# Experts of a decoder: the second norm moved into the middle stage, and the expert loop reordered

## The reference, cut to what matters

```python
scores = softmax(xf @ gate_w.T)                 # xf: 4096 x 128, the output of a layer norm
vals, idx = top_k(scores.T, k)                  # k = 512 tokens for each of 8 experts
y = xf[flat_idx].reshape(k, n, d)
mu = y.mean(-1, keepdims=True)
var = ((y - mu) ** 2).mean(-1, keepdims=True)
y = (y - mu) * rsqrt(var + LN_EPS) * ln_w + ln_b   # the second norm
h = gelu(einsum('knd,nfd->knf', y, fc1s) + b1s)
out = (einsum('knf,ndf->knd', h, fc2s) + b2s) * kept_w[..., None]
xf = xf.at[flat_idx].add(out.reshape(k * n, d))
```

## Time and profile before

| what | us |
|---|---|
| median of 3 runs (3424.35 to 3433.75) | 3430.83 |
| the profiled execution's own time | 3433.34 |
| its span, first to last instruction | 3430.7 |
| busy in the span: PE / DVE / ACT / POOL | 2574.6 / 1733.4 / 1027.6 / 342.9 |
| middle stage, one pass in its steady part | 103 |
| experts, first gather (1465.30) to the first load of the sum (1613.77) | 148.5 |

### The profile page before, as it was taken

The page is one execution under the profiler, slowest core; times in us unless marked ns, Lnnn a source line. Parts: engine busy times, 40 slices in busy tenths (PEclk is TensorE's granted clock), DMA queues, the critical chain, the costliest instruction groups (busy, mean ns, idle before and its releaser), DMA issues.

```text
span 3430.7 us, 54304 instructions
## 1 busy us (share of the span) xinstructions
PE 2574.6 (75%) x22608; PEld 1834.1 (53%) x22608; DVE 1733.4 (51%) x4213; ACT 1027.6 (30%) x1406; POOL 342.9 (10%) x580
## 2 busy tenths in 40 slices
PE   4666358888988886366777789777797777977778
PEld 3444146777777675244655454554545545454454
DVE  5555744566665654621367541575415754157540
ACT  3333422222222221021132442324423244232442
POOL 0111000000000000064111000110001100011000
PEclk8788658999999998588898999989999899998999
DMA  2000000000000001013700000000000000000000
GB/s 80 0 0 0 2 1 1 8 7 8 1 8 8 8 7 50 42 31 51 183 2 1 1 7 1 1 1 1 7 1 1 1 1 7 1 1 1 1 1 25
DMA packets 39364, 48.16 MB, mean 14 GB/s; under 512 B 7170, under 2 KB 36370, under 8 KB 38355
## 3 DMA queue, kind: packets, MB, share of 16 engines
q1 hardware_dynamic: 33490, 40.43, 4.0%
q0 software_dynamic: 5632, 4.33, 0.9%
HBM read 31.81 MB, written 12.91 MB: 13 GB/s over the span
## 4 chain that ended last, share of the span: by engine, by line
PE 42%; issue 32%; DVE 17%; POOL 4%; ACT 3%; DMA 1%; POOLq 0%; DVEq 0%; SPq 0%; ACTq 0%
PE banks L2332 6%; PE banks L861 5%; PE banks L2530 3%; PE banks L1361 2%; PE banks L1326 2%; PE banks L1160 2%; DVE weights L2053 2%; DVE xs L890 1%; PE banks L560 1%; PE banks L1394 1%; PE banks L2321 1%; POOL rstd L899 1%; PE banks L1106 1%; PE banks L1171 1%; PE banks L1952 1%
## 5 line engine op out<-in xcount | busy, mean ns | idle before, releaser
L2530 PE MATMUL banks<-wA 128*128 128x128 f32 x2234 | 302.2, 289 | 0.0
L2530 PEld LDWEIGHTS banks<-wA 128*128 128x128 f32 x2234 | 283.6, 203 | 15.0 <-issue 14.0
L882 DVE BATCH_NORM_STATS2 stats<-banks 128x6 f32<-128x128 f32 x208 | 46.3, 285 | 333.8 <-PE banks L861 295.2
L2224 DVE TENSOR_REDUCE wide_area<-banks 128x8 f32<-128x2048 f32 x64 | 146.6, 2291 | 102.9 <-PE banks L2144 102.9
L2196 ACT ACTIVATE weights<-banks 128x2048 f32<-128x2048 f32 x64 | 120.1, 1877 | 121.4 <-PE banks L2157 121.4
L897 POOL TENSOR_TENSOR rstd<-moments,eps 128x4 f32<-128x4 f32 x56 | 11.2, 201 | 1396.0 <-DVE moments L886 1396.0
L1717 DVE TENSOR_REDUCE wide_area<-banks 128x16 f32<-128x1024 f32 x80 | 94.1, 1218 | 54.1 <-PE banks L1630 53.8
L882 DVE BATCH_NORM_STATS2 dilvals<-banks 128x6 f32<-128x128 f32 x144 | 32.0, 285 | 174.6 <-PE banks L861 174.6
L890 DVE TENSOR_SCALAR xs<-banks,moments,rstd 128x128 f32<-128x128 f32 x208 | 71.0, 403 | 39.8 <-POOL rstd L899 39.3
L2332 PE MATMUL banks<-wide_area,big 128*128 128x512 f32 x192 | 86.3, 592 | 0.0
L922 ACT ACTIVATE xf<-banks 128x256 f32<-128x256 f32 x64 | 24.1, 384 | 205.8 <-PE banks L911 205.2
(11 more groups left out here) (746 smaller groups left out, 6165.9 us busy)
## 6 DMA issues: line engine op xcount, KB each, us to landing
big<-in_wE SPq DMA_DIRECT2D x1, 4096.0 KB, 12.5
weights<-long_kernel SPq DMA_DIRECT2D x8, 512.0 KB, 7.4
conv<-wide_area SPq DMA_DIRECT2D x16, 256.0 KB, 3.2
wC<-in_wC SPq DMA_DIRECT2D x1, 3012.0 KB, 17.4
wC<-in_wG SPq DMA_DIRECT2D x1, 2971.0 KB, 18.7
big<-in_wT SPq DMA_DIRECT2D x1, 2560.0 KB, 11.7
x_all<-in_xT SPq DMA_DIRECT2D x1, 2048.0 KB, 11.0
rows<-spread SPq DMA_DIRECT2D x8, 256.0 KB, 2.5
```

Of the source, the lines that this page charges most:

```text
L882: dve.bn_stats(m.stats[:, i, :], self.tokens(i)).then_inc(*sg.up("dve", f"stats{i}"))
L2224: dve.tensor_reduce(m.peaks[:, k % 2, :, :].rearrange("p t (r c) -> p r t c", r=4)[:, :, :, SPARE[j]], bank[:, :, :].rearrange("p r (t k) ...
L2530: pe.matmul(bank[:, 0:P], m.ident, m.ident, start=True, stop=True)
```

## The change

The second norm is taken out of the expert loop. In the middle stage a new class `LaneRows` makes the factor of the second norm from the moments of the first: a token that left the first norm has mean zero (taken as exactly zero now) and variance var x rstd x rstd. Four small operations on POOL make (var x rstd x rstd + eps) to the power -1/2, a fifth multiplies the tile of 512 tokens by it into `rows_normed`, and SP stores that into `rows_dram` in place of `far.xs`. `total_dram` still gets `far.xs`, now first. The lead lane's norm on DVE waits until POOL has read the moments that the two lanes share.

In the expert loop, `moments`, `root`, `scaled` and the copy of gate values are gone; `features` transposes the gathered rows themselves, and `weighted` reads the gate value from them. There are six buffers for gathered rows instead of three, five gathers are issued before the first add and one behind each of the first three adds. PE's order is features(0), features(1), hidden(0), hidden(1), features(2), and then `out(e)`, `hidden(e+2)`, `features(e+3)`, so that between the hidden layer of an expert and its output stands the work of another. ACT's order follows that. Twenty and five fillers stand before features(0) and features(1).

```diff
@@ class Experts
-    BUFFERS = 3
+    BUFFERS = 6
+    AHEAD = 5
...
+    def landed(self, e):
+        return self.gathered[e % self.BUFFERS], 16 * NT * (e // self.BUFFERS + 1)
...
         def gather(e):
             if e >= self.BUFFERS:
-                pool.wait_ge(*tk.done("dve", "weight", e - self.BUFFERS))
+                pool.wait_ge(*rs.done("dve", f"weighted{NT - 1}", e - self.BUFFERS))
...
-        def root(e):
...
-        gather(0)
-        gather(1)
-        root(0)
-        gather(2)
-        root(1)
+        for e in range(self.AHEAD):
+            gather(e)
         for e in range(EXPERTS):
-            if e + 3 < EXPERTS:
-                gather(e + 3)
-            if e + 2 < EXPERTS:
-                root(e + 2)
             add(e)
+            if self.AHEAD + e < EXPERTS:
+                gather(self.AHEAD + e)
...
         def features(e):
-            pe.wait_ge(*tk.done("dve", f"scaled{NT - 1}", e))
+            pe.wait_ge(*self.landed(e))
...
-        for e in range(2):
-            features(e)
-            hidden(e)
+        m.keep_busy(pe, m.S[0][:, 0, :], "taken")
+        features(0)
+        m.keep_busy(pe, m.S[0][:, 0, :], "chosen")
+        features(1)
+        hidden(0)
+        hidden(1)
+        features(2)
         for e in range(EXPERTS):
             out(e)
             if e + 2 < EXPERTS:
-                features(e + 2)
                 hidden(e + 2)
+            if e + 3 < EXPERTS:
+                features(e + 3)
...
+        affine(0)
+        affine(1)
+        gelu(0)
+        gelu(1)
+        affine(2)
+        for e in range(2, EXPERTS):
+            gelu(e)
+            if e + 1 < EXPERTS:
+                affine(e + 1)
...
-        def moments(e):
...
-        def scaled(e):
...
+                dve.tensor_scalar(m.weighted[e % 2][:, i, :], m.PT[:, e % 2, i * P:(i + 1) * P], self.taken(e)[:, i, D + e:D + e + 1],
                                   None, ALU.mult).then_inc(*rs.up("dve", f"weighted{i}"))
...
+class LaneRows:
+        self.sig = Section(clock, pool="part var eps root rows")
+    def pool(self, pool, n, scaled, written):
+        m, sg = self.lane, self.sig
+        pool.wait_ge(*scaled)
+        pool.tensor_tensor(self.factor, m.moments[:, :, 1], m.rstd, ALU.mult).then_inc(*sg.up("pool", "part"))
...
+        pool.tensor_tensor(self.factor, self.factor, m.rstd, ALU.mult).then_inc(*sg.up("pool", "var"))
...
+        pool.tensor_tensor(self.factor, self.factor, m.eps4[:, :], ALU.add).then_inc(*sg.up("pool", "eps"))
...
+        pool.tensor_tensor(self.factor, self.factor, m.minus_half[:, :], ALU.pow).then_inc(*sg.up("pool", "root"))
+        pool.wait_ge(*sg.done("pool", "root", n))
+        pool.wait_ge(*written)
+        pool.tensor_tensor(self.rows, m.xs, self.factor.unsqueeze(2).broadcast_to([P, NT, D]), ALU.mult).then_inc(*sg.up("pool", "rows"))
...
         def lead_dve(dve, it):
             yield from lead_down.dve(dve, it, m.big[:, :, bass.ds(it * T, T)])
+            if later(it, 2):
+                dve.wait_ge(*far_rows.sig.done("pool", "var", it - 2))
             yield from lead_norm.dve(dve, it, lead_down.z_ready(it))
...
             yield from far_norm.pool(pool, it)
+            far_rows.pool(pool, it, far_norm.sig.done("dve", f"scaled{NT - 1}", it), (saved, it * 48 + 16))
             yield from far_gate.pool(...)
...
             def store_rows(it):
                 sp.wait_ge(*far_norm.sig.done("dve", f"scaled{NT - 1}", it))
-                for dst, row in ((rows_dram, Experts.ROW), (total_dram, D)):
-                    sp.dma_start(..., far.xs[:, :, :]).then_inc(saved, 16)
+                sp.dma_start(bass.AP(total_dram.tensor, ...), far.xs[:, :, :]).then_inc(saved, 16)
+                sp.wait_ge(*far_rows.sig.done("pool", "rows", it))
+                sp.dma_start(bass.AP(rows_dram.tensor, ...), rows_normed).then_inc(saved, 16)
                 sp.wait_ge(*far_gate.sig.done("dve", "prob", it))
```

More of the change, by code:

```diff
@@ L494, in __init__ @@
         self.rows, self.total = rows, total
-        self.take = Signals(ctx, nc, "take", dve=tile_steps("stats", "aggr", "scaled") + " weight", pool="eps rstd", pe="features",
-                            act="out")
+        self.take = Signals(ctx, nc, "take", pe="features", act="out")
         self.hid = Signals(ctx, nc, "hidden", pe="h0 h1 h2 h3", act="g0 g1 g2 g3")
@@ L600, in gelu, with dve @@
                                bias=self.b1[:, e * FC + c:e * FC + c + 1]).then_inc(*hd.up("act", f"g{c}"))
-        for e in range(EXPERTS):
[L603 to L607, removed]
-        def moments(e):
[L610 to L616, removed]
-        def scaled(e):
[L619 to L625, removed]
-            dve.tensor_copy(m.token_weight[:, e, :], taken[:, :, D + e]).then_inc(*tk.up("dve", "weight"))
-        def weighted(e):
+        affine(0)
[7 more added lines that the diff above has]
+                affine(e + 1)
+    def dve(self, dve):
+        m, rs = self.mem, self.res
+        for e in range(EXPERTS):
             dve.wait_ge(*rs.done("pe", "o", e))
@@ L806 @@
 MIDDLE = "nfnfnfnfnfnfnfnfnfnffnfnfnnfnnfnnnffffnfnffnffnn"
-BUSY = {'first1': 2, 'dil_sum0': 7, 'wide scores1': 8, 'lead norm': 10, 'near norm': 1, 'dil_peaks1': 12, 'dil_peaks0': 2, 'lead product': 5, 'wide start': 2, 'gate': 7, 'back0': 3, 'first3': 1, 'first0': 1, 'last norm': 8, 'first norm': 6}
+BUSY = {'first1': 2, 'dil_sum0': 7, 'wide scores1': 8, 'lead norm': 10, 'near norm': 1, 'dil_peaks1': 12, 'dil_peaks0': 2, 'lead product': 5, 'wide start': 2, 'gate': 7, 'back0': 3, 'first3': 1, 'first0': 1, 'last norm': 8, 'first norm': 6, 'taken': 20, 'chosen': 5}
 MIDDLE_ALONE = "nnnnf" * 6
@@ L2474, in decoder @@
         m.index, m.slots = smalls[:, 0:32], smalls[:, 32:64].bitcast(U32)
-        m.token_weight = smalls[:, 64:64 + EXPERTS * NT].rearrange("p (e i) -> p e i", i=NT)
-        m.taken = [cross_keys[:, i * NT * Experts.ROW:(i + 1) * NT * Experts.ROW].rearrange("p (i d) -> p i d", d=Experts.ROW)
-                   for i in range(Experts.BUFFERS)]
-        m.normed = [m.xs, m.states[:, :].rearrange("p (i d) -> p i d", d=D)]
+        takers = [(cross_keys, i) for i in range(3)] + [(gate_blocks, i) for i in range(3)]
+        m.taken = [x[:, i * NT * Experts.ROW:(i + 1) * NT * Experts.ROW].rearrange("p (i d) -> p i d", d=Experts.ROW) for x, i in takers]
         m.chosen = [m.af[:, :], m.qf[:, :]]
@@ L2869, in decoder @@
         far_norm = LaneNorm(clock, far)
+        far_rows = LaneRows(clock, far, rows_normed, rows_factor)
         far_gate = LaneGate(clock, far, w["gate_w"])
```

34 lines of the change are left out of this document (14 added, 20 removed).

## The result

The changed kernel takes 3406.64 us in the median (3395.24 to 3409.28), the kernel before 3430.83 beside it (3420.81 to 3440.02): a ratio of 0.9924, 95% interval 0.991 to 0.9938. That is 24.2 us faster, where 31.8 were forecast; 3406.6 lies inside the range of 3389 to 3411. The profiled execution took 3409.28 us, with a span of 3407.5 and a granted clock of 0.899.

The account below looks back on a forecast made before the run. Before, a serial chain with PE waiting for DVE bound the experts, next POOL's issuing. Loop gain 28.0 us and start 3.7, middle stage 0, give 31.7, so 3399 us from the median 3430.83; range 3389 to 3411.

Parts of the forecast that it names:

- POOL as the next bound: Expert loop: POOL's adds and gathers set the pace, 85.1 us from first add to load, was 113.1; gain 28.0.
- The rule weighed against it: Expert loop: the skill calls descriptor generation small; the prediction sided with the trace, four adds 7.62 us, four gathers 5.0.
- the first rival: Expert loop: POOL's issue is cheaper than it looks, PE sets the end; 8.6 us more gain, 3390; 5%.
- PE's need: Expert loop: PE needs out 6.0, hidden 3.70 and features 0.67 per expert, 10.4 us, below POOL's 12.6.
- The start: First gather to first add: first add at 1497.0 against 1500.69, 3.7 us gained, from 1.3 to 5.7.
- the five gathers don't delay it: Ahead of the first add: the twentieth gather is issued at 1491.3 and POOL is free a microsecond later.
- The middle stage: Eight passes: LaneRows fits POOL's idle stretch, 2.9 to 4.4 us each, cost 0; upper bound 23 to 35.
- The sum: Whole kernel: load of the sum at 1582.1 in place of 1613.77, 31.7 us earlier; 3399 from the median.
- what follows moves with it: After the experts: later work waits for the load of the sum, so it comes 31.7 us earlier too.
- The rivals: Whole kernel: cheaper POOL issue 3390, 5%; middle stage pays, 4%; PE at 1.2 GHz 3465, 4%; partial 3410 to 3420, 7%.
- The clock in the experts: Experts, rival: PE stays at 1.2 GHz, 20.1 us per expert, slower than before at 3465; 4%.
- the passes didn't pay: Middle stage, rival: POOL reaches the gate copies late, 23 to 35 us cost, 3422 to 3434; 4%.

Follow-up runs that it names:

- old_order: Changed kernel with the earlier PE and ACT order (features and hidden of one expert together, no fillers): 3403.60 us, ratio 0.9922 to the kernel before.
- pe_filler: Changed kernel with eight fillers on PE ahead of each expert output from expert 1 on: 3407.92 us, ratio 0.9935 to the kernel before.
- ahead6: Changed kernel with six experts' gathers ahead of the first add in place of five: 3407.64 us, ratio 0.9924 to the kernel before.
- spread: Changed kernel with six experts' gathers first, then half an expert's gathers behind each of the first four adds: 3407.41 us, ratio 0.9918 to the kernel before.
- ahead4: Changed kernel with four experts' gathers ahead of the first add in place of five: 3413.76 us, ratio 0.9936 to the kernel before.
- no_lane_rows: Changed kernel without LaneRows, rows stored without the second norm: 3404.40 us, ratio 0.9926 to the kernel before.

## Why the prediction was right, and where its size was off

- **POOL as the next bound**: right. Forecast were three steps of 12.6, four of 9.59 and 8.85, 85.1 us; measured 12.65 three times, then 9.72, 10.23, 9.65 and 9.56, and 8.87, 85.97. What supports the cause, beyond the agreement, are old_order (no change), pe_filler (later only where the gathers have run out) and ahead6 and spread (shorter by the gathers taken out of the loop).
- **The rule weighed against it**, the Trainium skill's "small, variable" for descriptor generation ("DMA: Bandwidth & Descriptors", section "Anatomy of one DMA — SWDGE (gpsimd) path"), is the one by which the first rival would have come, 3390. The trace disagrees: four adds still take 1509.84 - 1502.30 = 7.54 us with no root between them, and four gathers 5.1.
- **PE's need**: 10.4 forecast, 9.88 measured, at a granted clock of 1.00. Its order and its waits for ACT cost nothing in the loop, because all of it lies below 12.65 and PE has won a lead of 7.6 us by add(3), on which the steps of 9.6 behind it draw. The 10.4 assumed the new order, and at five gathers first the old one with its 11.01 does as well. So the gain comes from the norm that no longer stands between a gather and its features, and from the deeper lead of the gathers. ahead4 tells them apart: its gathers and adds stand in POOL's queue in the order of before (four first, then one behind each of the first four adds), and first add to load takes 89.93 us where before took 113.1. So 23 of the 27 us come without a deeper lead, with the norm out of the loop (PE's order brought nothing with five ahead, and the six buffers were not tried by themselves), and 4 with the fifth gather ahead.
- **The start**: 31.7 forecast, 32.6 measured, and that it came so near is luck in part: two errors nearly cancel. features(1) ended at 1483.90, 14.2 us behind the first gather, as forecast; hidden(0) took 3.60 in place of the 5.7 that the sum left for it (31.7 - 14.2 - 3.70 - 0.67 - 7.46), so that out(0) began 7.2 us behind features(1) where the sum had 10.0; and from the start of out(0) at 1491.13 to the first add were 11.2 us where 7.46 had been carried over from the earlier trace rows. The gaps take 2.4 of these 3.7, slower matmuls around them the rest. The 3.60 is no effect of the fillers to count on, as shown above; in pe_filler and no_lane_rows, with 4.94, the gaps are shorter and the first add comes at 32.5 and 32.4. The step "the five gathers don't delay it" is the one that failed: it looked at POOL's queue only.
- **The middle stage**: cost 0 forecast, and shown for passes with the same clock. The end of `LaneRows`, 3.05 us behind the scaling, lies in the range of 2.9 to 4.4. The product took 1.04 us where 1.27 had been taken from L2288. That line is not of the same form, as the prediction had it: it is an addition, of one row of 128 values to each of the four tiles, where `LaneRows` multiplies by one factor for each token.
- **The sum**: 31.7 us forecast, 29.9 in the stage, 24.2 in the median. The 1.8 us are the two terms of 0.9 above. The other 5.7 lie outside the stage (6.7 in the two profiled executions, 4.4 ahead of it and 2.3 behind). Of the 4.4, the middle stage has 2.9, 721.1 against 718.2: its one long pass. The step "what follows moves with it" holds for the order of the work but not to some microseconds: among nine other kernels whose program up to the experts is that of the changed one (without old_order, where four passes of 109.2 us put it at 1485.79), the first gather comes between 1464.65 and 1472.41, and from the load to the end takes from 1813.0 to 1823.0. One execution of before, at 1465.30 and 1816.9, was a favourable one to start from on the first count. The forecast allowed some 5 us each way for this; no step of the change is shown to cost them, nor is it shown that `LaneRows` has no part in the long passes.
- **The rivals**: none came. The clock in the experts was 0.88, hidden layers ran in 3.60 us except the one behind the gaps (5.74), and the passes didn't pay but for the one in which the clock fell late (2.3 us).

## What to carry to other kernels

When a stall is taken out of one engine's path, add up the next engine's needs in full before the gain is named, issues and the gaps between them included: here that gave the new spacing to 0.1 us and the loop to 0.9. A reordering can be worth 7 us of a stage or nothing, by whether another engine is slower; and it can need another edit as its condition, as more than three gathers ahead are needed here to keep a kernel from losing 80 us (with four the stage is 2 us longer). Work put in a stretch where its engine is shown idle can be free, and whether it is can be told by comparing passes under the same clock rather than medians.

## What the runs showed of the hardware

A row-wise gather of 128 rows held POOL for 0.95 us and an accumulating one for 1.55, with 0.30 us to the next; four take 5.1 and 7.5 us, and by this the loop was bound. With the gathers of five or six experts issued back to back, PE stood still for stretches of 0.2 to 2.1 us with no wait that the profile shows; with five the last of them ended at most 29.9 us behind the first gather, with six at most 35.3, and with three and four there were none. With five and six, PE's signal to ACT that features(2) is done came 2.0 to 5.1 us behind the end of its record in the new order (0.8 with four). The cause isn't known. A sixth gather issued into 5.68 us in which POOL is idle moved the first add by 5 us, more than the 3.6 that it won later. The same hidden layer behind the same fillers ran at a granted clock of 1.00 in two traces and at 0.68 to 0.73 in six.
